# Attention with two key tiles in every run of values products: diagonal tiles placed between the off-diagonal ones, sums of exponentials in single pieces

## What is computed

```python
qg = q.reshape(b, s, NKV, g, D)
logits = jnp.einsum('bqhgd,bkhd->bhgqk', qg, k) * scale
causal = jnp.tril(jnp.ones((s, s), bool))
logits = jnp.where(causal, logits, jnp.float32(-1e+30))
w = jax.nn.softmax(logits, axis=-1)
out = jnp.einsum('bhgqk,bkhd->bqhgd', w, v).reshape(b, s, NQ * D)
return out @ Wo + bo
```

## Time and profile before

| | |
|---|---|
| time, median of 3 runs | 1179.27 us (1178.64 to 1185.39) |
| span of the profiled execution | 1192.9 us (the page gives its span alone, no time beside it) |
| TensorE busy | 1101.2 us, 92% |
| VectorE busy | 850.0 us, 71% |
| GpSimd busy | 587.1 us, 49% |
| ScalarE busy | 551.1 us, 46% |
| chain of work that ended last | TensorE 76%, VectorE 14%, issue 3%, the rest 7% |
| values products in the chain (L1490) | 19%, its largest line |

### The profile page before, as it was taken

The page is one execution under the profiler, slowest core; times in us unless marked ns, Lnnn a source line. Parts: engine busy times, 40 slices in busy tenths (PEclk is TensorE's granted clock), DMA queues, the critical chain, the costliest instruction groups (busy, mean ns, idle before and its releaser), DMA issues.

```text
span 1192.9 us, 16695 instructions
## 1 busy us (share of the span) xinstructions
PE 1101.2 (92%) x5727; PEld 661.8 (55%) x5727; DVE 850.0 (71%) x1752; ACT 551.1 (46%) x1155; POOL 587.1 (49%) x635
## 2 busy tenths in 40 slices
PE   3799999999999999999999999999999986888993
PEld 2455555554565555545655555456555552477893
DVE  5777978777779787777797877777878785464343
ACT  2445544544455445454544454545444443553451
POOL 5544645645356456453564564635544337125441
PEclk9879999999999999999999999999999998899997
DMA  8000000000000000000000000000010003132104
GB/s 229 15 1 1 1 2 1 1 1 1 1 1 1 1 1 2 1 1 1 1 1 1 1 1 1 1 1 1 3 70 1 1 3 120 37 83 73 39 26 119
DMA packets 30017, 25.08 MB, mean 21 GB/s; under 512 B 4480, under 2 KB 25344, under 8 KB 29936
## 3 DMA queue, kind: packets, MB, share of 16 engines
q1 hardware_dynamic: 26224, 18.45, 5.5%
q0 software_dynamic: 2272, 4.72, 1.2%
q10 hardware_dynamic: 1440, 0.85, 0.2%
HBM read 15.62 MB, written 8.40 MB: 20 GB/s over the span
## 4 chain that ended last, share of the span: by engine, by line
PE 76%; DVE 14%; issue 3%; ACT 2%; DMA 2%; POOL 1%; another core or an unknown queue 1%; ACTq 0%; SPq 0%; DVEq 0%; POOLq 0%
PE PS L1490 19%; PE PS L1443 12%; PE PS L1472 12%; PE PS L1474 9%; PE PS L1574 3%; DVE part_max L1067 3%; PE PS L1418 3%; PE PS L1598 2%; PE PS L1540 2%; PE PS L1456 2%; PE PS L1425 2%; PE PS L1514 2%; DVE full L1085 2%; PE PS L1446 1%; PE PS L1585 1%
## 5 line engine op out<-in xcount | busy, mean ns | idle before, releaser
L1067 DVE TENSOR_REDUCE part_max<-PS 128x1 f32<-128x512 f32 (+2 forms) x576 | 340.0, 618 | 125.2 <-PE PS L1443 101.8
L831 ACT ACTIVATE full<-PS 128x512 f32<-128x512 f32 x384 | 223.5, 598 | 217.9 <-PE PS L1474 193.1
L1472 PE MATMUL PS<-store 128*128 128x512 f32 (+3 forms) x640 | 275.5, 431 | 13.0 <-issue 8.3
L1443 PE MATMUL PS<-store 128*128 128x512 f32 (+3 forms) x640 | 250.9, 417 | 8.8 <-ACT store L811 3.4
L1474 PE MATMUL PS<-store 128*128 128x512 f32 (+3 forms) x640 | 236.0, 369 | 0.0
L669 POOL TENSOR_TENSOR full<-full 128x512 f32<-128x512 f32 x120 | 155.4, 1326 | 138.6 <-PE PS L1490 137.5
L840 ACT ACTIVATE diag<-PS 128x512 f32<-128x512 f32 (+3 forms) x256 | 111.3, 441 | 209.1 <-PE PS L1477 174.6
L1443 PEld LDWEIGHTS PS<-store 128*128 128x128 f32 x640 | 119.5, 192 | 144.1 <-DVE part_max L1067 62.0
L1490 PE MATMUL PS<-full,V 128*64 128x512 f32 x768 | 194.0, 616 | 0.0
L699 POOL TENSOR_TENSOR lower<-lower 128x320 f32<-128x320 f32 x64 | 60.2, 941 | 258.6 <-DVE lower L1045 257.1
L1472 PEld LDWEIGHTS PS<-store 128*128 128x128 f32 x640 | 124.9, 195 | 89.8 <-issue 27.0
(11 more groups left out here) (228 smaller groups left out, 1500.4 us busy)
## 6 DMA issues: line engine op xcount, KB each, us to landing
lower<-in_L_ffn_experts_w_dram SPq DMA_DIRECT2D x16, 256.0 KB, 4.3
sent<-full SPq DMA_DIRECT2D x1, 2574.0 KB, 11.9
full<-sent SPq DMA_DIRECT2D x9, 264.0 KB, 7.3
lower<-made SPq DMA_DIRECT2D x8, 256.0 KB, 4.9
full<-in_L_attn_x_dram SPq DMA_DIRECT2D x2, 512.0 KB, 7.3
out_dram<-XA SPq DMA_DIRECT2D x4, 256.0 KB, 2.7
made<-lower,back_to POOLq DMA_INDIRECT x39, 2.2
wo_sb<-in_L_attn_Wo_dram SPq DMA_DIRECT2D x1, 512.0 KB, 10.7
```

Source lines behind the costliest of these rows:

```text
L831: nc.scalar.activation(full[:, k % QUADS, r, :], PS[:, bank, :], ACT.Exp).then_inc(probs_ready, 1)
L1067: nc.vector.reduce_max(part_max[:, t, b:b + 1], PS[:, bank, 0:width], AX.X).then_inc(ring_dve, 1)
L1443: last = nc.tensor.matmul(PS[:, bank, 0:w], QT[:, ch % 2, h, t * P:(t + 1) * P], KT[:, 0, keys:keys + w], start=True, stop=not last_bank)
L1472: nc.tensor.matmul(o, KT[:, 0, keys:keys + P], QT[:, ch % 2, h, q0:BANK], start=True, stop=False)
```

## The change

The off-diagonal and diagonal key tiles of a pair step are put into one order with a diagonal tile as the second of a run (`runs_of`, `ORDER`), for chunk 3: (0,0) (0,1) | (0,2) d0 | (0,3) (1,0) | (1,1) d1 | (1,2) (1,3) | (2,0) d2 | (2,1) (2,2) | (2,3) d3. Every run of values products holds two key tiles. A run of chunk 0 holds two diagonal tiles. The additions for the sums come as single pieces straight behind the run whose tiles they add (`sums_after`), each with its own wait and its own signal. A diagonal piece goes to the tile with the same r that has been made last by then (`diag_into`), and so in the last chunk d0 goes to q = 0, d1 and d2 to q = 1, d3 to q = 2: the first three are GpSimd's now (`diagadd`), only d3 is VectorE's (`diagsum`).

```diff
+    def runs_of(ch):
+        on = [(ch, r) for r in range(TB)]
+        off = [(q, r) for q in range(ch) for r in range(TB)]
+        if ch == 0:
+            return [on[0:2], on[2:4]]
+        runs = []
+        for r in range(TB):
+            ahead = {1: 1, 2: 3 if r % 2 else 1, 3: 3}[ch]
+            tiles, off = off[:ahead], off[ahead:]
+            tiles.append(on[r])
+            runs += [tiles[k:k + 2] for k in range(0, len(tiles), 2)]
+        return runs
...
+    def diag_into(ch, r):
+        upto = ORDER[ch][:(ORDER[ch].index((ch, r)) // 2 + 1) * 2]
+        return max([q for q, t in upto if t == r and q < ch], default=0)
+
+    def sums_after(J, run):
...
+            if 0 < q < ch:
+                kind = "quadsum" if q == CHUNKS - 2 else "poolsum"
+                items += [(kind, J, m, q, r) for m in range(2)]
...
+                kind = "diagsum" if diag_into(ch, r) == CHUNKS - 2 else "diagadd"
+                items += [(kind, J, m, r) for m in range(2)]
...
-        for q in range(J // PAIRS + 1):
-            for r in range(TB):
+        for run in RUNS[J // PAIRS]:
+            for at, (q, r) in enumerate(run):
                 main += [("s", J, q, r, 0), ("s", J, q, r, 1)]
-                if q < J // PAIRS and r % 2 == 0:
-                    main.append(("gap", 2.1 * len(pending)))
+                if at:
+                    main.append(("gap", 2.1 * at))
                 else:
                     main += pending
...
+            pending = [("pv", J, q, r) for q, r in run] + sums_after(J, run)
...
-        place(diag_steps(6) + tail_steps(6), 7.0, 7.48),
+        place(tail_steps(6), 7.15, 7.48),
...
+                    elif x[0] == "diagadd":
...
+                            pool.wait_ge(pv_done, n.at["pv", J, q, r] + 1)
+                            if q:
+                                pool.wait_ge(pool_added, n.at["poolsum", J, m, q, r] + 1)
+                            acc = full[:, quad_of[J, m, q] % QUADS, r, r * P:BANK]
+                            last = nc.gpsimd.tensor_tensor(acc, acc, diag[:, m, r, r * P:BANK], ALU.add)
...
+                        last.then_inc(diag_pool, 1)
...
                     dve.wait_ge(pv_done, n.at["pv", J, q, k] + 1)
                     if q > 1:
-                        if ("poolsum", J, m, q - 1) in n.at:
-                            dve.wait_ge(pool_added, n.at["poolsum", J, m, q - 1] + 1)
+                        if ("poolsum", J, m, q - 1, k) in n.at:
+                            dve.wait_ge(pool_added, n.at["poolsum", J, m, q - 1, k] + 1)
...
+                    if ("diagadd", J, m, k) in n.at:
+                        dve.wait_ge(diag_pool, n.at["diagadd", J, m, k] + 1)
```

## The result

The changed kernel takes 1214.18 us (median of 4 runs, 1210.51 to 1217.70), the kernel before 1179.60 beside it: 1.0289 times as long, interval 1.0259 to 1.0319. It is slower by 34.6 us where 14 us faster was forecast, and outside the range.

The account below looks back on a forecast made before the run. TensorE's issue was taken to set the attention's time. Fewer runs 17.6 us, less 1.2 where TensorE waits anyhow and 2 for scores in a row, gave 14.4 us less: 1165 against the median 1179.27, range 1155 to 1184.

Parts of the forecast that it names:

- Fewer runs: On TensorE in the attention, 160 runs of values products instead of 220 save boundary costs: 17.6 us less.
- Additions in single pieces: Diagonal additions cut up, six per last-chunk pair step moved from VectorE to GpSimd; costed at nothing, VectorE's 25% spare covering it.
- Scores in a row: TensorE's scores wait for exponentials where three or more stand together; 0 to 3.6 us lost, 2 taken.
- More waits: ScalarE and GpSimd look at a semaphore for each piece instead of each quad; costed at nothing, at most 2 us.
- Rival 1: Side work at hand-set fractions shifts against the main line and TensorE's waits eat the gain; 1168 to 1190, chance 0.24.
- Rival 2: In the last chunk VectorE waits for GpSimd's diagonal piece, 5.5 us in each of seven pair steps; 1200, chance 0.10.
- Rival 3: ScalarE's unnamed 10 us wait in the last pair step shrinks or goes; 1160 with half, 1155 with all, chance 0.09.
- Rival 4: A run's boundary is paid by each head's pair of products, so nothing changes; 1179, chance 0.03.

Follow-up runs that it names:

- e12_thin_sums: Changed kernel with GpSimd's diagonal additions of chunks 1 to 3 and VectorE's sums of four into one cut to one column; 1174.3 us, ratio 0.994.
- e6_thin: Changed kernel with GpSimd's diagonal additions of chunks 1 to 3 cut to one column, instructions, waits and places kept; 1187.7 us, ratio 1.008.
- e11_thin3: Changed kernel with only the last chunk's diagonal additions on GpSimd cut to one column; 1203.2 us, ratio 1.022.
- b0_before: The kernel before, unchanged, run again for a second profile; 1177.8 us.
- e13_before_thin: Kernel before with the same cuts to one column as e12_thin_sums, in its own order of tiles; 1164.8 us, ratio 0.990.
- e7_place: Kernel before's tile order with additions in single pieces, GpSimd's diagonal pieces of chunks 0 to 2 where its blocks stood; 1180.2 us, ratio 1.001.
- e5_gaps_before: Kernel before with 4.2 units more of gap in each pair step, so only the side work's places move; 1191.5 us, ratio 1.012.
- e2_sums: Kernel before's tile order and engines, but additions in single pieces, each behind its product; 1202.7 us, ratio 1.022.
- e1_order: Changed kernel with the last chunk's diagonal pieces given back to VectorE, still as single pieces; 1205.5 us, ratio 1.022.
- e3_gaps: Changed kernel with gap weights scaled so each pair step has its old notional length; 1201.6 us, ratio 1.020.
- e10_memset: Changed kernel with GpSimd's diagonal additions of chunks 1 to 3 replaced by memsets of about equal time; 1191.3 us, ratio 1.009.

## Why the prediction was wrong, step by step

**Fewer runs: the mechanism was right, the credit was not.** Each run is as long as forecast. With equal cuts the changed order saves TensorE 5.1 us of busy time in two groups, where 17.6 us over four groups had been written, 8.8 for two. The runs' own length alone gave 6.2 us in two groups (136.4 to 130.2), so the 0.15 to 0.21 us a run that were credited for getting in and out do not show. And a saved microsecond counts only where nothing else ends last. That was the step from the earlier trace rows: 97% busy in the middle was read as "what TensorE issues sets the time". In e12_thin_sums most of what TensorE saved became idle time.

**Additions in single pieces: costed at nothing, and this is the step that failed.** The time that GpSimd's new places cost VectorE stood at 0 in the sum; VectorE's two-input time grew by 32.7 us. The prediction saw the contention in the earlier trace rows, priced it for the 42 pieces moved in the last chunk, and let VectorE's 25% of spare time cover it. Two things were wrong. The pieces of chunks 1 and 2, which stay on their engine, were not priced at all, since nothing about them seemed to change; but they leave their block at the start of a pair step and are spread to where VectorE sums. In the three groups e6_thin is 16.1 us shorter than the changed kernel and e11_thin3, with the moved pieces alone cut, 2.0; the other 14.1 are theirs, less what the blocks of before had cost. The moved pieces weigh in the last four pair steps, where e11_thin3 takes off 5.8 us and e6_thin 8.2. And the 25% is an average. In the kernel before (b0_before) VectorE is busy 9.93 of 10 us from 120 us on, and again from 360, 600 and 840 us on, the same place of the later groups. There is no cover in such a stretch. One place of the changed kernel, with pieces of chunk 2 on GpSimd:

```profile
441.65 2.80 POOL L709 TENSOR_TENSOR full<-full,diag 128x512 f32<-128x512 f32 x2 [0.24 <-POOL lower L735]
```

and VectorE beside it:

```profile
441.99 1.29 DVE L1086 TENSOR_TENSOR store<-lower,store 128x64 fp32r<-128x64 f32 x1
443.21 1.79 DVE L1143 TENSOR_TENSOR full<-full 128x512 f32<-128x512 f32 x1
...
446.32 0.67 DVE L1143 TENSOR_TENSOR full<-full 128x512 f32<-128x512 f32 x1
```

Alone the two take 0.22 us (L1086 at 328.90) and 0.67 (L1143 at 446.32).

**Scores in a row.** The 2 us were not lost: TensorE waits no longer for exponentials than before, also where it waits less for VectorE (3.2 us in e12_thin_sums, 3.8 in e13_before_thin).

**More waits: right**, as far as the number of waits goes. e7_place has the pieces and their waits, and the time of before.

**Rival 1 named the right thing and bounded it wrongly.** The hand-set fractions shift, and e5_gaps_before shows 14 us for that alone. The bound, "TensorE's waits double", had no ground in a row: they went from 20.8 to 43.3 us, and the rival left out that in the changed order the shift brings VectorE's sums and GpSimd's additions together. It had 0.24 and ended at 1190.

**Rival 2 had the sign and not the place.** In the changed kernel VectorE waits 6.0 us for GpSimd's additions (1.5 and 1.1 in the groups shown, 3.4 ahead of maxima), not 38. In the old order (e2_sums), though, its mechanism is just what costs, for the pieces at a pair step's end, which it had not looked at.

**Rival 3** is out: the wait was not the kernel's (b0_before). **Rival 4** is out by the rows of the runs.

**The end.** The last pair step takes 34.50 us, before 34.79; the one before it grew from 56.44 to 61.52. In the latter VectorE normalises nine tiles for the router, in the changed kernel beside GpSimd's additions (983.04 to 987.51):

```profile
982.87 5.74 DVE L980 TENSOR_SCALAR lower<-XA,moments,rstd 128x128 f32<-128x128 f32 x9
```

In b0_before it does eight of them in 2.14 us:

```profile
955.17 2.14 DVE L950 TENSOR_SCALAR lower<-XA,moments,rstd 128x128 f32<-128x128 f32 x8
```

TensorE waits 4.5 us for VectorE behind it (the row of L1552 among its waits). GpSimd's sends follow that chain and end behind the last scores, so TensorE waits for the fetch, in the changed kernel

```profile
1050.99 1.08 PE L1593 MATMUL PS<-ident,full 128*128 128x128 f32 x4 [4.37 <-DMA full<-sent]
```

and in the kernel before (b0_before)

```profile
1017.18 0.63 PE L1562 MATMUL PS<-ident,full 128*128 128x128 f32 x4 [2.35 <-DMA full<-sent]
```

**What adds up and what stays open.** With GpSimd's diagonal pieces thin, the three groups take 718.0 us, the time of before; with them 734.1. That is the size of the groups' 15.5 us, and the last four pair steps come to 158.6, under the 160.2 of before. How much of it the kernel before would have gained by the same cut alone is not shown; with the sums cut besides, the two orders lie within 2 us of each other in the groups (707.7 changed, 709.5 before), so the groups' loss goes when the additions and the sums that meet them go. None of this says why the three groups are not 13 us shorter. Idle time in the changed order takes the gain back, at other places in each variant, for instance ahead of the query maxima in pair step 4 of each group (L1487 for part_max, 6.2 us in four places, still 3.6 in e6_thin); which rule of placing would avoid it was not found. Of the opening's 9.3 us, some are scatter between executions: with the instructions of the changed kernel there, e11_thin3 has 139.6 us at a mean granted clock of 0.95, the changed kernel 144.0 at 0.93, e1_order 145.5 at 0.89. So it is not shown that e3_gaps takes off 4.3 of them and e6_thin 4.9. e12_thin_sums still has 7.4 against its control: why the opening is longer is not settled.

## What to carry to other kernels

A saving on the busiest engine is worth what the second busiest has to spare in that stretch, not on average: look at VectorE's busy time in slices of 10 us before crediting TensorE. An addition that stays on its engine is not free when it moves in time: ask which two-input work of VectorE GpSimd's new place falls beside, and what stands ahead of it in GpSimd's queue. And a cut that shows a gain needs the same cut in the old kernel beside it: e12_thin_sums without e13_before_thin would have told a wrong story.

## What the runs showed of the hardware that was not expected

GpSimd's memsets leave VectorE's two-input additions (L1145 of e10_memset) at 0.68 us, where in the changed kernel GpSimd's additions raise those beside them to 0.96 on average. VectorE's maxima, which read PSUM, take 685 ns in the changed kernel as in the kernel before, whatever GpSimd does. A stretch is not always a factor of the instruction's size: 64 columns, 0.22 us alone (L1086), took 1.29 us beside an addition of GpSimd, as in the earlier trace rows. And VectorE's normalisation, with one large input in SBUF (L980), was stretched as well, from 0.27 us a tile to 0.64 (b0_before and the changed kernel, in the part on the end).
